# A patch embedding, a Mamba-style block and a mixture of experts in one kernel: the bounds of the experts' linear part go from VectorE to ScalarE

## What is computed

```python
def _swiglu(h):                       # ALPHA, LIMIT = 1.702, 7.0
    x_glu, x_lin = jnp.split(h, 2, axis=-1)
    x_glu = jnp.minimum(x_glu, LIMIT)
    x_lin = jnp.clip(x_lin, -LIMIT, LIMIT)
    return x_glu * jax.nn.sigmoid(ALPHA * x_glu) * (x_lin + 1.0)

g = t @ gate_w.T + gate_b
vals, idx = jax.lax.top_k(g, K)
w = jax.nn.softmax(vals, axis=-1) / K
full_w = jnp.zeros((T, E), jnp.float32).at[jnp.arange(T)[:, None], idx].set(w)
h = _swiglu(jnp.einsum('th,ehf->tef', t, w1) + b1)
y = jnp.einsum('tei,eih->teh', h, w2) + b2
out = jnp.einsum('teh,te->th', y, full_w) * K
```

## Time and profile before

| What | Value |
|---|---|
| Median of 3 runs | 626.87 us (625.98 to 630.05) |
| The profiled execution | 627.44 us, of which the span from the first to the last instruction is 625.6 us |
| Mean granted clock of PE | 0.945 of full speed |
| Busy PE, PEld | 557.0 us (89% of the span), 479.1 us (77%) |
| Busy DVE, ACT, POOL | 475.5 us (76%), 295.2 us (47%), 388.3 us (62%) |
| DMA | 88.34 MB, mean 141 GB/s |

### The profile page before, as it was taken

How to read it: one execution, slowest core, us unless ns; L and a number is a source line. 1 busy time by engine, 2 the same in 40 slices (tenths; PEclk the granted TensorE clock), 3 DMA queues, 4 the chain that set the end, 5 groups by cost and what they waited for, 6 DMA issues and landing times.

```text
span 625.6 us, 10398 instructions
## 1 busy us (share of the span) xinstructions
PE 557.0 (89%) x3361; PEld 479.1 (77%) x3361; DVE 475.5 (76%) x897; ACT 295.2 (47%) x699; POOL 388.3 (62%) x447
## 2 busy tenths in 40 slices
PE   3959589977899999989999997999998889978896
PEld 3748478866698988879887885988886768857785
DVE  1166868889789789979879996999989556565664
ACT  1167846483544475544446474445442324323442
POOL 3257777767456458857555984767677355564674
PEclk9779959989899999999999997999999889997999
DMA  9993533432053343413343341554342266553781
GB/s 238 308 299 97 164 119 90 189 135 92 1 155 100 106 155 95 162 33 112 111 171 112 105 141 46 135 157 143 121 177 88 50 207 213 178 174 104 238 274 52
DMA packets 41827, 88.34 MB, mean 141 GB/s; under 512 B 9581, under 2 KB 34477, under 8 KB 35501
## 3 DMA queue, kind: packets, MB, share of 16 engines
q1 hardware_dynamic: 41772, 87.68, 43.4%
HBM read 77.24 MB, written 10.40 MB: 140 GB/s over the span
## 4 chain that ended last, share of the span: by engine, by line
PE 61%; DVE 15%; issue 6%; DMA 6%; ACT 5%; POOL 4%; SPq 2%; POOLq 0%; DVEq 0%; ACTq 0%
PE post L770 12%; PE y_sum L770 10%; PE sums L770 10%; PE gate_up L770 10%; PE pre L770 8%; PE linear_up L770 8%; DVE state L1255 4%; DMA w<-w_store 3%; PE fills L770 3%; DVE fills L1246 2%; DVE dts L1222 2%; SPq L709 1%; POOL read L1456 1%; DMA hid<-patches 1%; DVE scratch L1354 1%
## 5 line engine op out<-in xcount | busy, mean ns | idle before, releaser
L1456 POOL TENSOR_TENSOR read<-state,c_all 128x504 f32<-128x504 f32 (+1 forms) x120 | 147.0, 1228 | 83.2 <-DVE state L1255 54.8
L1255 DVE TENSOR_TENSOR_SCAN state<-a_bar,fills 128x504 f32<-128x504 f32 (+1 forms) x120 | 133.0, 1109 | 12.1 <-ACT a_bar L1035 4.1
L1485 POOL TENSOR_TENSOR scratch<-scratch 128x252 f32<-128x252 f32 (+1 forms) x120 | 81.6, 680 | 87.4 <-DVE scratch L1369 82.4
L770 PE MATMUL y_sum<-read,ident 128*128 128x252 f32 (+1 forms) x480 | 122.5, 382 | 4.1 <-POOL read L1456 3.7
L1035 ACT ACTIVATE scratch<-scratch 128x252 f32<-128x252 f32 (+1 forms) x120 | 47.3, 394 | 147.0 <-DVE scratch L1354 146.8
L770 PE MATMUL sums<-hid,w 128*128 128x252 f32 (+1 forms) x480 | 103.8, 377 | 4.8 <-POOL hid L1494 4.8
L770 PE MATMUL gate_up<-t_high,w 128*128 128x252 f32 (+1 forms) x360 | 89.3, 318 | 14.5 <-DVE route L1332 7.2
L770 PEld LDWEIGHTS y_sum<-read,ident 128*128 128x128 f32 x480 | 86.3, 201 | 19.8 <-issue 7.1
L1035 ACT ACTIVATE a_bar<-dts,decay 128x245 f32<-128x245 f32 (+1 forms) x240 | 100.2, 470 | 2.2 <-DVE dts L1230 2.2
L1494 POOL TENSOR_TENSOR hid<-scratch,route_rows 128x252 f32<-128x252 f32 (+1 forms) x120 | 84.9, 708 | 14.4 <-DMA route_rows<-mix_rows 7.6
L770 PE MATMUL linear_up<-t_high,w 128*128 128x252 f32 (+1 forms) x360 | 85.8, 308 | 2.3 <-ACT mix_w L1035 1.7
(11 more groups left out here) (166 smaller groups left out, 851.9 us busy)
## 6 DMA issues: line engine op xcount, KB each, us to landing
w<-w_store SPq DMA_DIRECT2D x40, 1152.0 KB, 5.7
route_rows<-mix_rows SPq DMA_DIRECT2D x192, 63.0 KB, 3.0
w_store<-w SPq DMA_DIRECT2D x8, 1152.0 KB, 5.0
scratch<-expert_w SPq DMA_DIRECT2D x16, 384.0 KB, 5.6
w<-expert_w SPq DMA_DIRECT2D x1, 2304.0 KB
route_rows<-mix_rows SPq DMA_DIRECT2D x48, 36.0 KB, 2.8
w_embed<-embed_w SPq DMA_DIRECT2D x3, 256.0 KB, 3.9
x_patch<-patches SPq DMA_DIRECT2D x1, 756.0 KB, 5.0
```

The lines of the kernel that those rows point to most:

```text
L770: return nc.tensor.matmul(out, lhsT, rhs, start=start, stop=stop, skip_group_check=shared, is_transpose=turned)
L1255: dve.tensor_tensor_scan(pair(state, i, c), pair(a_bar, i, c), pair(fills, i, c), 0.0, ALU.mult, ALU.add).then_inc(scanned.sem, 1)
L1456: pool.tensor_tensor(by_state(pair(read, i, c)), by_state(pair(state, i, c)), c_all[:, n:n + 2, 0:tok(c)], ALU.mult).then_inc(read_out.sem, 1)
L1485: pool.tensor_tensor(glu[:, 0:tok(c)], product[un % 2][:, 0:tok(c)], g_one[un % 2][:, 0:tok(c)], ALU.mult)\
```

## The change

Both bounds of the linear part become rectifications on ScalarE. With u the linear part without its bias, `x_under` makes `l_under = relu((7 - b) - u)` and `x_low` makes `l_min = relu(14 - l_under)`, which is the bounded linear part plus 7; `x_gated` then adds -6 where it took the maximum with -6. `x_linear` and `x_turn` now wait for `x_under`. In the order, `x_under(un-1)` stands ahead of `x_gate(un)` and `x_low(un-1)` behind it; `x_gated(un-1)` and `x_glu(un-1)` go behind `x_min(un)`, in the turn of `x_linear(un)`; `x_scale(un-2)` goes into the turn of `x_gate(un)`. The planner gets new costs, spans and a higher weight of waits, so all streams are interleaved anew.

```diff
         first, second = [("x_gate", un)], [("x_linear", un), ("x_min", un), ("x_tanh", un), ("x_one", un)]
         if un:
-            first += [("x_low", un - 1), ("x_gated", un - 1), ("x_glu", un - 1)]
-            second += [("x_scale", un - 1)]
+            first = [("x_under", un - 1)] + first + [("x_low", un - 1)]
+            second[3:3] = [("x_gated", un - 1)]
+            second += [("x_glu", un - 1)]
+        if un > 1:
+            first.append(("x_scale", un - 2))
...
-    unit_turns += [[("x_low", last), ("x_gated", last), ("x_glu", last)], [("x_scale", last)]]
+    unit_turns += [[("x_under", last), ("x_low", last), ("x_scale", last - 1), ("x_gated", last), ("x_glu", last)],
+                   [("x_scale", last)]]
...
-WAIT_WEIGHT = 0.5
-BEFORE_SPAN = 15.5
-AFTER_SPAN, LAST_AFTER_SPAN = 20.9, 22.0
-EXPERT_SPAN, LAST_EXPERT_SPAN = 25.1, 21.7
+WAIT_WEIGHT = 1.6
+BEFORE_SPAN = 18.33
+AFTER_SPAN, LAST_AFTER_SPAN = 21.97, 15.37
+EXPERT_SPAN, LAST_EXPERT_SPAN = 24.01, 21.82
...
+            def x_under(c, un):
+
+                act.wait_ge(pe_linear.sem, pe_linear.at(c, un + 1))
+                activate(l_under[:, 0:tok(c)], half(linear_up, c, 0), ACT.Relu, scale=-1.0, bias=col("b1_linear", un))\
+                    .then_inc(linear_under.sem, 1)
+
+            def x_low(c, un):
+
+                act.wait_ge(linear_under.sem, linear_under.at(c, un + 1))
+                if un:
+                    act.wait_ge(gated.sem, gated.at(c, un))
+                activate(l_min[:, 0:tok(c)], l_under[:, 0:tok(c)], ACT.Relu, scale=-1.0, bias=bounds[:, 0:1])\
+                    .then_inc(linear_min.sem, 1)
...
-            def x_low(c, un):
-                dve.wait_ge(pe_linear.sem, pe_linear.at(c, un + 1))
-                if un:
-                    dve.wait_ge(gated.sem, gated.at(c, un))
-                dve.tensor_scalar(l_min[:, 0:tok(c)], half(linear_up, c, 0), col("b1_linear", un),
-                                  1.0 + LIMIT, ALU.add, ALU.min).then_inc(linear_min.sem, 1)
-
             def x_gated(c, un):
...
                 dve.scalar_tensor_tensor(product[un % 2][:, 0:tok(c)], l_min[:, 0:tok(c)], 1.0 - LIMIT,
-                                         g_min[un % 2][:, 0:tok(c)], ALU.max, ALU.mult).then_inc(gated.sem, 1)
+                                         g_min[un % 2][:, 0:tok(c)], ALU.add, ALU.mult).then_inc(gated.sem, 1)
...
-                    pool.tensor_scalar(linear, linear, 1.0, None, ALU.add).then_inc(bias_raised.sem, 1)
+                    pool.tensor_scalar(linear, linear, -1.0, LIMIT, ALU.mult, ALU.add).then_inc(bias_turned.sem, 1)
```

More of the change, by code:

```diff
@@ L220, in rests_on @@
 def rests_on(c, step, i):
-    if step in ("x_gate", "x_linear", "x_min", "x_tanh", "x_one", "x_low", "x_gated", "x_glu", "x_scale", "x_down"):
-        return {"x_gate": [("x_min", i - 1)], "x_linear": [("x_low", i - 1)], "x_min": [("x_gate", i)],
-                "x_tanh": [("x_min", i)], "x_one": [("x_tanh", i)], "x_low": [("x_linear", i)],
+    if step in ("x_gate", "x_linear", "x_min", "x_tanh", "x_one", "x_under", "x_low", "x_gated", "x_glu", "x_scale", "x_down"):
+        return {"x_gate": [("x_min", i - 1)], "x_linear": [("x_under", i - 1)], "x_min": [("x_gate", i)],
+                "x_tanh": [("x_min", i)], "x_one": [("x_tanh", i)], "x_under": [("x_linear", i)], "x_low": [("x_under", i)],
                 "x_gated": [("x_low", i), ("x_min", i)], "x_glu": [("x_gated", i), ("x_one", i)],
@@ L359 @@
     "x_start": (("P", .85),), "x_gate": (("P", .6),), "x_linear": (("P", .6),), "x_min": (("V", .43),),
-    "x_tanh": (("S", .33),), "x_one": (("S", .4),), "x_low": (("V", .41),), "x_gated": (("V", .34),),
+    "x_tanh": (("S", .33),), "x_one": (("S", .4),), "x_under": (("S", .38),), "x_low": (("S", .38),), "x_gated": (("V", .34),),
     "x_glu": (("G", .68),), "x_scale": (("G", .68),), "x_down": (("P", .47),), "x_finish": (("V", 1.2),),
@@ L412, in vit_tower @@
         ones = sb("ones", [P, 1])
+        bounds = sb("bounds", [P, 1])
         after_wait = sb("after_wait", [HM, 1])
@@ L489, in vit_tower @@
         g_tanh, glu, l_min = piece(0), piece(1), piece(2)
+        l_under = sb("l_under", [P, TM])
         g_min, g_one, product = (piece(3), piece(4)), (piece(5), piece(6)), (piece(7), piece(8))
@@ L512, in vit_tower @@
         in_halved = signal("in_halved", 0)
-        bias_raised = signal("bias_raised", 0)
+        bias_turned = signal("bias_turned", 0)
         picks_rounded = signal("picks_rounded", 0)
@@ L597, in vit_tower @@
         gate_min = signal("gate_min", UNITS)
+        linear_under = signal("linear_under", UNITS)
         linear_min = signal("linear_min", UNITS)
@@ L948, in x_logits @@
                 if not c:
-                    pe.wait_ge(bias_raised.sem, 1)
+                    pe.wait_ge(bias_turned.sem, 1)
                 else:
@@ L961, in x_turn @@
                 if c:
-                    pe.wait_ge(linear_min.sem, linear_min.at(c - 1, UNITS))
+                    pe.wait_ge(linear_under.sem, linear_under.at(c - 1, UNITS))
                 pe.wait_ge(route_steps.sem, route_steps.at(c, 10))
@@ L1004, in x_linear @@
                 if un:
-                    pe.wait_ge(linear_min.sem, linear_min.at(c, un))
+                    pe.wait_ge(linear_under.sem, linear_under.at(c, un))
                 else:
@@ L1171, in _ @@
                  "square3": square3, "t_high": t_high_copy, "x_exp": x_exp, "x_mix": x_mix,
-                 "x_tanh": x_tanh, "x_one": x_one})
+                 "x_under": x_under, "x_low": x_low, "x_tanh": x_tanh, "x_one": x_one})
         @block.vector
@@ L1398, in _ @@
                  "center3": center3, "roots3": roots3, "scale3": scale3,
-                 "x_topk": x_topk, "x_route": x_route, "x_min": x_min, "x_low": x_low, "x_gated": x_gated,
+                 "x_topk": x_topk, "x_route": x_route, "x_min": x_min, "x_gated": x_gated,
                  "x_finish": x_finish})
@@ L1497, in _ @@
             pool.memset(ones[:, :], 1.0)
+            pool.memset(bounds[:, :], 2.0 * LIMIT)
             pool.memset(minus_half[:, :], -0.5)
```

## The result

| | Before | After |
|---|---|---|
| Median | 626.61 us (4 runs, 625.98 to 630.05) | 649.32 us (4 runs, 646.19 to 654.75) |
| Ratio | | 1.036, 95% interval 1.027 to 1.045 |
| Span of the profiled execution | 625.6 us | 649.6 us |
| Busy DVE, ACT | 475.5, 295.2 us | 423.5, 391.7 us |

A forecast was written before the change was run, and what follows sets the result against it. The prediction took PE's matmuls to bound the kernel for most of its time. Its terms, -6 - 2.5 - 0.4 + 2.8 + 3.3 + 0 + 0 = -2.8 us, gave 624.6 profiled, a median of 624.0; range 611 to 638.

The forecast's parts named there:

- A2: Routing of cut 2: collects and `outproj` matmuls ahead of `x_turn` fill PE's gap; -2.5 us, between 0 and -4.2.
- B: Routing of cut 3: `x_turn` comes 1.8 us earlier, against a later end of cut 2's experts; -0.4 us net.
- F: First 170 us, ahead of the experts: only the planner's order changes; 0, between -4 and +4 us.
- R2: Rival: in the last cut later `hid` delays SyncE's route loads and the weight loads behind them; median 638.0 us, chance 0.19.
- A: Middle, 170 to 480 us: VectorE's relief shortens PE's waits; -6 us, between -14 and 0.
- R3: Rival: the change frees nothing on VectorE, as its two-input operations grow as long as the relief; median 629.5 us, chance 0.10.
- R1: Rival: VectorE was the bound of the middle, so its relief brings more; median 613.2 us, chance 0.36.
- C: End of a cut's experts: a unit's chain is 1.4 us longer, bare after cuts 3 and 4; +2.8 us.
- D: Last cut: later `hid` holds SyncE's route loads, so six weight loads come later; +3.3 us, between 0 and +7.
- E: Tail, 572 to 617 us: ScalarE, at 40.9 of 45 us, has room for the added instructions; 0, between 0 and +2.

The follow-up runs named there:

- edit_both: Changed kernel with the old constants, a pair's weight load ahead of the route loads in the last cut, cut 3's patches behind the expert weights: 628.22 us, ratio 1.005.
- before_both: Kernel before with the same two SyncE loads moved (last cut's weights, cut 3's patches): 623.50 us, ratio 0.996.
- weights_first: Changed kernel with the old constants; in the last cut SyncE issues a pair's weight load ahead of the route loads: 627.54 us, ratio 1.003.
- turn_first: Changed kernel with the first 518 steps of before; in cuts 1 and 2 the experts' steps up to `x_turn` go first: 639.50 us, ratio 1.021.

## Why the prediction was wrong

The sum that was measured, in medians, taken apart step by step: 649.32 - 637.04 = 12.3 us is the order up to the first routing, 637.04 - 630.43 = 6.6 the order behind it, 630.43 - 626.61 = 3.8 the edit (4.7 against the runs of before made beside it). No term of the prediction had the 6.6: A2 and B took two places out of the new order behind the routing, and the rest stood at nothing. What it hangs on stays open.

- **F is the step that failed.** The prediction said of the first 170 us "Only the planner's order changes" and "I find no sign: 0, between -4 and +4". It was +15.8 in the trace, and 12.3 in the run that puts the old order back. There is no experts' work there, and yet the change acts, by an order that the planner makes without knowing what a DMA costs: `split_w1` has a price on ScalarE and GpSimd in its table and none for its load. The step rested on the experts' part of the order alone. SyncE's order, which is the same in both kernels, would not have shown it either: what shrank is the distance between the step that a load waits for (cut 2's embedding) and the step that needs it (the 14th piece on ScalarE). Moving the load gave back 8.8 of the 12.3 us, as uncertain as said above; putting the piece back to its old place on ScalarE wasn't tried, and what the rest hangs on is open. In the forecast SyncE was the cause of a loss as well (R2), but in the last cut and by another pair of loads. None of the signs that were to show the forecast wrong lay in this stage.
- **A was wrong, in size and sign.** Forecast -6, between -14 and 0. VectorE's busy time did fall as forecast:

```profile
170.00:480.00 310.00, 298.10 (x1879) 261.88 (x1878) 244.90 (x423) 207.51 (x504) 203.92 (x231) 0.98 0.38 122
```

This is the kernel with the old constants: 244.90 us against 274.38, 79% of the stretch, so R3 (nothing is freed) falls. But from `x_turn` of cut 0 to the logits of cut 3 it takes 315.3 us where before takes 313.7, and `edit_both` is above `before_both`. That VectorE was full in 14 slices did not mean that it was waited for: PE was full there too. That was R1's counterargument, and R1 falls with A. What PE waited for from 170 to 480 us (us in total, times, longest), before and then with the old constants:

```profile
PE gate_up L770 <- DVE scratch L1354: 1.7, 3, 0.7
...
PE sums L770 <- POOL hid L1494: 1.3, 2, 0.8
...
PE linear_up L770 <- DVE scratch L1361: 0.6, 2, 0.4
```

```profile
PE sums L777 <- POOL hid L1508: 3.3, 3, 1.4
...
PE linear_up L777 <- ACT mix_w L1042: 1.1, 1, 1.1
PE pre L777 <- ACT c_all L1042: 1.0, 1, 1.0
PE pre L777 <- ACT us L1042: 0.6, 1, 0.6
PE gate_up L777 <- DVE scratch L1375: 0.2, 1, 0.2
```

Only 2.3 us of PE's idle time were waits for `x_min` and `x_low`, and the edit took 2.1 of them away. In exchange PE waits 2.0 us longer for `hid` (1.9 and 3.2 us in all in `edit_both` and `weights_first`) and 2.7 us for ScalarE, for which the trace of before lists no wait. A counted all of the idle time outside the routing as a wait for VectorE and put at nothing, in this stage, what the longer chain and the fuller ScalarE add. How much of that is the chain and how much the new order wasn't separated.

- **A2 had the right place.** The wait of 1.26 us ahead of `fills` is gone, and by `turn_first` the work in the gaps of cuts 1 and 2 is worth 2.5 us against leaving them empty; against the order of before, which A2 was about, its size wasn't measured.
- **B was right in its mechanism**, its net size wasn't measured. In the routing of cut 3, after:

```profile
506.05 0.19 DVE L1367 TENSOR_TENSOR route<-route,route_sum 126x32 f32<-126x32 f32 x1
```

```profile
506.39 0.38 PE L973 MATMUL linear_up<-ident,route 126*16 126x126 f32 x2 [0.52 <-DVE route L1367]
```

`x_turn` follows the weights by 0.15 us, where it was 1.86.
- **C was right for one unit's chain.** The last unit after, as the earlier trace rows for before:

```profile
638.58 0.48 DVE L1375 TENSOR_SCALAR scratch<-gate_up,vec 128x252 f32<-128x252 f32 x1 [1.14 <-PE gate_up L777]
...
640.97 0.42 DVE L1383 SCALAR_TENSOR_TENSOR scratch<-scratch 128x252 f32<-128x252 f32 x1 [1.58 <-ACT scratch L1042]
```

```profile
641.47 0.71 POOL L1499 TENSOR_TENSOR scratch<-scratch 128x252 f32<-128x252 f32 x1 [0.49 <-DVE scratch L1383]
642.26 0.71 POOL L1508 TENSOR_TENSOR hid<-scratch,route_rows 128x252 f32<-128x252 f32 x1
```

From the end of the last `x_min` (639.06) to the last `hid` (642.97) it is 3.9 us; forecast 4.0, before 2.63. That it would be hidden in the steady state is not what the middle shows, where PE's waits for `hid` rose.
- **D had the right place, and its size was too large.** The loads are 6.6 us apart on average after (594.92 to 628.08, five intervals), but they were 6.2 before (574.41 to 605.38): the 5.91 of the earlier trace rows was one interval and not the mean. PE's wait for weights rose by 1.4 us with the old constants (2.4 to 3.8), not by 3.3.
- **E was right:** ScalarE has 35.45 of 45 us in the tail (40.9 was forecast), and PE waits there for `l_under` once, 0.4 us.

The sentence drawn from the Trainium skill, "ScalarE: Activation LUTs", section "Rules for kernel authors" (VectorE rather than ScalarE for simple arithmetic), had the right sign here, though not because of the price of one instruction: 0.44 us on ScalarE against 0.45 on VectorE.

## What to carry to other kernels

Where a planner's constants change, compare the whole order on every queue, also in stages that the change doesn't touch. For each load look at what its issue waits for and at what needs it, and at how much work stands between the two: the queue of the loads can be the same in both kernels while that distance shrinks. Relief for an engine is worth something only in stretches where another engine waits for it; count that wait, not the busy share, and count what the move adds to other waits. When an operation moves to another engine, draw the ring of the loop with each engine's own order in it, since one edge of that order can cost more than the operation.

## What the runs showed of the hardware

Short waits of PE had a second price. After 1.8 us of waiting for a `y` step at 257.6 us the granted clock of the changed kernel was 0.5 (1.2 GHz) for 3.4 us, and in the wait of 5.2 us that ended at 121.2 it fell to 0.5 at 117.7 and stayed there until 128.0. The same kernel's runs differ by 8.6 us (646.19 to 654.75), the longer ones at the lower mean clock, where the runs of before lie within 4.1 us.
